# First attention: a head's maxima are turned into a row one step later, between that step's scores and values

## The chip, the cores and the metric

The kernel runs on one core of a Trainium2 chip. The metric is device time in microseconds (us) of one execution. Three executions of the kernel before took 3412.55, 3414.42 and 3423.49 us; their median, 3414.42 us, is the time before.

The core has five engines that run side by side and meet at semaphores: TensorE (PE, with its weight loads shown as PEld), VectorE (DVE), ScalarE (ACT), GpSimd (POOL) and SyncE (SP), which here only issues DMAs.

## The reference

The program is two transformer layers. Each layer is an attention and a feed-forward part, both with layer norms and residuals around them. Only the first attention is touched:

```python
B, S, H, NH = 2, 1024, 512, 16          # head width HD = 32
q, k, v = (proj(Wq), proj(Wk), proj(Wv))
q = q * cos + rotate_half(q) * sin      # k likewise
scores = jnp.einsum('bhqd,bhkd->bhqk', q, k) / math.sqrt(HD)
scores = jnp.where(causal, -jnp.inf, scores)
attn = jax.nn.softmax(scores, axis=-1)
out = jnp.einsum('bhqk,bhkd->bhqd', attn, v)
```

There are 32 heads (2 batches of 16) of 1024 queries by 1024 keys.

## The kernel before, in words

The first attention, `attention_layer0` (its tiles carry the prefix `l0a_`), treats one head after another. A head is worked on three times:

- **Maxima ("M").** The scores of a 128-query block are computed with the queries on the partitions, in parts of up to 512 keys: 12 parts in a head, widths 128, 256, 384, 512, 512+128, 512+256, 512+384, 512+512. PE writes a part into one of the two slots of `mbank` (L938, the causal mask by L941), and DVE reduces it to the negated maximum of each query (L1017). After the 12th part DVE joins the two halves of the blocks 4 to 7 into `negmax` (L1020, "the join").
- **The row ("N").** `negmax` is 128 x 8. PE transposes it (L948) into the next slot of `mbank`, DVE splits the 8 x 128 result into a rounded part and a rest (L1026, L1028), and SP copies both by DMA into two rows of `q_stack` (L894, L896). Against two rows of ones in `k_stack` they subtract each query's maximum inside the matmul.
- **Scores, exponentials, values ("Z", "L", "P", "O").** A head has six units. Z (L957, mask L960) computes a unit's scores with the keys on the partitions into one of two slots of `sbank`; ACT takes their exponential twice (L994 rounded, L995 in full); L on POOL subtracts one from the other for the rest (L1067, in four units of six); P (L981) multiplies with the values into `obank`; O on DVE copies and adds the finished half (L1036, L1039).

The order of the work is a list of steps, `steps_layer0`; each engine walks through the same list and does its own share. A head has six steps (k = 0 to 5). Step i does the scores of unit i + 2, the exponential rest of unit i, the values of unit i - 3, the copies that have become ready, and two maxima parts of the head after next. So during head h the row of head h + 1 is made (its maxima were finished in the last step of head h - 1), and the twelve maxima parts of head h + 2. The scores of head h + 1 start in step k = 4 of head h; they wait for the two DMAs of the row, which SP issues at its k = 2.

Two waits matter for what follows. The transpose waits for the join and for every reduction that stands before it in the list (`wait(pe, m_done, use["N", n])`). A maxima part waits until the part two places before it in the two slots of `mbank` has been reduced; the row takes one place in that sequence too.

Once in a group of four heads DVE inverts the group's sums (L1006), in the last step before its copies, and POOL then scales the group's output with them (L1058, twice), in step k = 1 of a head.

Of the kernel before, what the change touches and what calls it, by code (L numbers as in the profile page):

```python
# [734 lines left out]
HEADS = B * NH  # L735
# [31 lines left out]
def steps_layer0():  # L767

    for i in range(FIRST, LAST):
        h, k = divmod(i, U)  # L770
        if 0 <= i + 2 < HEADS * U:
            yield "Z", i, i + 2
        if k == 0 and 0 <= h + 1 < HEADS:
            yield "N", i, h + 1
        if 0 <= i < HEADS * U:
            yield "L", i, i
        p, o = i - LAG, i - LAG - 1
        if 0 <= p < HEADS * U:
            yield "P", i, p
        if 0 <= o < HEADS * U and o % U in (1, U - 1):  # L780
            yield "O", i, 2 * (o // U) + (o % U == U - 1)
        if h + 2 < HEADS:
            yield "M", i, 2 * (h * U + 2 * U + k)
            yield "M", i, 2 * (h * U + 2 * U + k) + 1


def uses_layer0():

    out, n = {}, 0
    for kind, _, e in steps_layer0():  # L790
        if kind in "MN":
            out[kind, e] = n
            n += 1
    return out


def attention_layer0(nc, m, ident, ident_bf, mask, qk_dram, v_dram, v32_dram, sums_dram, inverse_dram, out, next_load):
# [34 lines left out]
    with nc.Block() as block:  # L832
# [93 lines left out]
        def _(pe):  # L926
            pe.wait_ge(rows_set, 1)
            for kind, i, n in steps_layer0():
                if kind == "M":
                    h, part = divmod(n, len(MAX_PARTS))  # L930
# [54 lines left out]
        @block.scalar  # L985
        def _(act):
            for kind, i, n in steps_layer0():
                if kind == "Z":
                    _, _, wide = pieces(n % U)
                    r = n % RING0  # L990
                    act.wait_ge(scores_full, n + 1)
                    wait(act, values_done, n - RING0 + 1)
                    if n % U not in IN_FP32:
                        nc.scalar.activation(probs_hl[:, r, 0, 0:wide], sbank[:, n % 2, 0:wide], ACT.Exp)  # L994
                    nc.scalar.activation(probs[:, r, 0:wide], sbank[:, n % 2, 0:wide], ACT.Exp).then_inc(exp_done, 1)  # L995
# [1229 lines left out]
```

## Time and profile before

| | |
|---|---|
| median of three executions | 3414.42 us |
| profiled execution, its time | 3422.34 us |
| profiled execution, its span | 3420.6 us |
| PE busy over the span | 2878.7 us (84%) |
| DVE busy | 1944.4 us (57%) |
| ACT busy | 1184.9 us (35%) |
| POOL busy | 942.8 us (28%) |
| first attention | from 213 us to about 677 us of the span |
| mean granted TensorE clock | 0.927 |

Shares of the span are means over stages that are bound by different engines. The first attention fills slices 3 to 8 of the 40 of the page. A span that the trace calls busy on PE is modelled at its end; starts are what is measured, and intervals below are from start to start where that is possible.

### The profile page before, as it was taken

To read this page: it belongs to the slowest core of one execution; us is meant where nothing else is said; L and a number is where in the kernel's file an instruction comes from. 1 tells how busy PE (TensorE), PEld (TensorE's weight loads), DVE (VectorE), ACT (ScalarE), POOL (GpSimd) and SP (SyncE) were. 2 spreads that over 40 slices of the span, in tenths; PEclk is the share of its full clock that TensorE was granted. 3 is DMA by queue.
4 is the path that set the end of the run, shared out by engine and by line. 5 is a ranking of instruction groups with operands and counts; after the bars stand their busy time and mean duration, and the time that the engine had idled before them with its cause. 6 is when DMAs were issued, how large, how long until landed. Compare 5 with 4: busy or idle time off the path is not lost. (4 is left out here: it accounts for less than half of the span.)

```text
span 3420.6 us, 42283 instructions
## 1 busy us (share of the span) xinstructions
PE 2878.7 (84%) x14636; PEld 2300.5 (67%) x14636; DVE 1944.4 (57%) x3582; ACT 1184.9 (35%) x2287; POOL 942.8 (28%) x664
## 2 busy tenths in 40 slices
PE   7968888778999997358999999489999993588994
PEld 6846566556888885237888888468888882466773
DVE  5647777582223323345666666556666666766755
ACT  2226555532111111132444444224444442233331
POOL 1226666651111112104000000240000002277633
PEclk9979999988999998689999999799999996799997
DMA  4764333121100001760000000300000003111002
GB/s 171 238 190 123 112 106 110 48 99 56 37 19 19 18 1 64 245 270 27 22 21 32 21 32 17 151 27 22 21 32 21 32 17 135 37 37 37 0 1 98
DMA packets 123391, 236.96 MB, mean 69 GB/s; under 512 B 12832, under 2 KB 67104, under 8 KB 122496
## 3 DMA queue, kind: packets, MB, share of 16 engines
q1 hardware_dynamic: 123264, 235.32, 20.7%
q8 instruction: 73, 1.20, 0.2%
q14 instruction: 54, 0.44, 0.0%
HBM read 162.14 MB, written 72.88 MB: 69 GB/s over the span
## 5 line engine op out<-in xcount | busy, mean ns | idle before, releaser
L1067 POOL TENSOR_TENSOR l0a_probs_hl<-l0a_probs,l0a_probs_hl 128x896 fp32r<-128x896 f32 (+1 forms) x128 | 285.8, 2242 | 161.5 <-ACT l0a_probs L995 161.5
L1299 PE MATMUL l1a_obank<-l1a_pT_hl,l1k_v_hl 128*128 128x512 f32 (+3 forms) x1152 | 300.4, 370 | 7.2 <-DVE l1a_pT_hl L1372 7.1
L1372 DVE TENSOR_TENSOR l1a_pT_hl<-l1a_work,l1a_pT_hl 128x512 fp32r<-128x512 f32 (+3 forms) x384 | 213.1, 555 | 155.1 <-ACT l1a_pT_hl L1332 154.9
L1325 ACT ACTIVATE l1a_probs<-l1a_scores,l1a_row 128x128 f32<-128x128 f32 (+7 forms) x256 | 189.3, 741 | 318.0 <-DVE l1a_row L1362 318.0
L1279 PE MATMUL l1a_scores<-l1k_kT_hl,l1a_qa_hl 128*128 128x512 f32 (+3 forms) x1152 | 291.8, 362 | 1.5 <-ACT l1a_probs L1325 1.5
L1415 POOL TENSOR_TENSOR l1a_q_stage<-l1k_qpe,l1a_ones 128x512 fp32r<-128x512 f32 x32 | 33.3, 1040 | 875.9 <-PE l1a_work L1307 818.4
L1704 DVE TENSOR_TENSOR f0f_hid<-f0f_silu,f0f_ubank 128x512 f32<-128x512 f32 x64 | 44.1, 689 | 319.6 <-PE f0f_ubank L1639 319.6
L1332 ACT CAST l1a_pT_hl<-l1a_work 128x512 fp32r<-128x512 f32 (+3 forms) x384 | 183.5, 478 | 107.3 <-PE l1a_work L1290 106.1
L1307 PE MATMUL l1a_work<-l1a_wov,l1a_oT_hl 128*128 128x512 f32 x768 | 214.1, 401 | 5.0 <-DVE l1a_oT_hl L1391 3.0
L1362 DVE TENSOR_REDUCE l1a_row<-l1a_scores 128x1 f32<-128x128 f32 (+7 forms) x256 | 189.8, 751 | 44.7 <-PE l1a_scores L1282 44.6
L1759 POOL TENSOR_TENSOR f0f_h_hl<-f0f_hid,f0f_h_hl 128x512 fp32r<-128x512 f32 x64 | 82.7, 1292 | 475.6 <-ACT f0f_h_hl L1676 475.6
L1386 DVE SCALAR_TENSOR_TENSOR l_acc<-l1a_work,l1a_row,l_acc 128x512 f32<-128x512 f32 x256 | 189.4, 750 | 34.5 <-PE l1a_work L1307 25.3
L1279 PE MATMUL l1a_scores<-l1k_kpe,l1a_q_stack 128*128 128x512 f32 (+3 forms) x768 | 203.4, 346 | 0.0
L1279 PEld LDWEIGHTS l1a_scores<-l1k_kT_hl,l1a_qa_hl 128*128 128x128 f32 x1152 | 188.8, 191 | 21.7 <-ACT l1a_probs L1325 1.8
L1299 PEld LDWEIGHTS l1a_obank<-l1a_pT_hl,l1k_v_hl 128*128 128x128 f32 x1152 | 181.6, 191 | 28.8 <-DVE l1a_pT_hl L1372 14.9
L1290 PE MATMUL l1a_work<-all_ident,l1a_probs 128*128 128x128 f32 x1152 | 192.2, 276 | 9.5 <-DVE l1a_qa_hl L1377 6.2
L1639 PE MATMUL f0f_gbank<-x_xT,f0f_wT 128*128 128x512 f32 x768 | 190.6, 397 | 1.4 <-DVE f0f_wT L1698 1.4
L994 ACT ACTIVATE l0a_probs_hl<-l0a_sbank 128x896 fp32r<-128x896 f32 (+1 forms) x128 | 124.3, 971 | 190.1 <-PE l0a_sbank L957 115.9
L1649 PE MATMUL f0f_ybank<-f0f_wT,f0f_h_hl 128*128 128x512 f32 x768 | 189.8, 396 | 0.1
L1639 PE MATMUL f0f_ubank<-x_xT,f0f_wT 128*128 128x512 f32 x768 | 189.3, 395 | 0.0
L1649 PE MATMUL f1f_ybank<-f1f_wT,f1f_h_hl 128*128 128x512 f32 x512 | 139.6, 417 | 55.3 <-DVE f1f_h_hl L1708 36.4
L1290 PEld LDWEIGHTS l1a_work<-all_ident,l1a_probs 128*128 128x128 f32 x1152 | 140.6, 141 | 47.9 <-DVE l1a_qa_hl L1377 12.8
(258 smaller groups left out, 6255.3 us busy)
## 6 DMA issues: line engine op xcount, KB each, us to landing
v_dram<-l0f_v_rows SPq DMA_DIRECT2D x24, 768.0 KB, 4.3
qk_dram<-l0f_stage SPq DMA_DIRECT2D x128, 128.0 KB, 2.5
l1a_wov<-wov_dram SPq DMA_DIRECT2D x32, 512.0 KB, 3.4
l0a_v_stage<-v_dram SPq DMA_DIRECT2D x32, 384.0 KB, 4.3
l1a_wabs<-wabs_dram SPq DMA_DIRECT2D x32, 384.0 KB, 3.8
l0a_q_stack<-qk_dram SPq DMA_DIRECT2D x32, 256.0 KB, 3.5
l0a_k_stack<-qk_dram SPq DMA_DIRECT2D x32, 256.0 KB, 3.9
wov_dram<-w1a_wov SPq DMA_DIRECT2D x16, 512.0 KB, 3.3
```

The source lines that it names most:

```text
L1067: nc.gpsimd.tensor_tensor(probs_hl[:, r, 1, 0:wide], probs[:, r, 0:wide], f32(probs_hl[:, r, 0, 0:wide]), ALU.subtract).then_inc(low_done, 1)
L1279: last = pe.matmul(scores[:, buf, cols], lhs, rhs, start=(i == 0), stop=(not diagonal and i == len(steps) - 1))
L1290: last = pe.transpose(work[:, slot, i * P:(i + 1) * P], probs[s][:, first + n, :], ident[:, :])
L1299: last = pe.matmul(obank[:, c:SPAN], src["v_hl"][:, a, n, :], pT_hl[:, ring(n, s), b, c:SPAN], start=(n == 0 and i == 0), stop=(n == QT * ...
L1307: last = pe.matmul(work[:, slot, :], oT_hl[:, s, a, n * P:(n + 1) * P], wov[:, hp, b, :], start=(i == 0), stop=(i == 2))
L1325: nc.scalar.activation(probs[s][:, first:first + wide, :].rearrange("p k c -> p (k c)"), scores[:, n % S_AHEAD, 0:wide * P], ACT.Exp, bias ...
L1332: nc.scalar.copy(pT_hl[:, ring(n, s), 0, c:SPAN], work[:, slot, c:SPAN]).then_inc(turned_high, 1)
L1362: nc.vector.tensor_reduce(row[:, 0, row_slot:row_slot + 1], scores[:, n % S_AHEAD, 0:wide * P], AX.X, ALU.max, negate=True).then_inc(max_d ...
L1372: nc.vector.tensor_tensor(pT_hl[:, r, 1, c:SPAN], work[:, slot, c:SPAN], f32(pT_hl[:, r, 0, c:SPAN]), ALU.subtract).then_inc(work_free[slo ...
L1386: nc.vector.scalar_tensor_tensor(out=out[:, t, :], in0=work[:, slot, :], scalar=row[:, 2, row_slot:row_slot + 1], in1=out[:, t, :], op0=AL ...
L1639: last = pe.matmul(bank[:, b, :], wT[:, half, wa, w, c * HG + b * P:c * HG + (b + 1) * P], xT_hl[:, xa, c, a * SPAN:(a + 1) * SPAN], start ...
L1649: last = pe.matmul(ybank[:, b % 2, :], h_hl[:, a % 2, ht, ha, b * P:(b + 1) * P], wT[:, half, wa, 2, ht * D:(ht + 1) * D], start=(n == 0), ...
```

## The change

One line of the list of steps: the row of head h + 1 is yielded in step k = 1 of head h instead of step k = 0. Within a step it keeps its place, behind the scores and ahead of the values.

```diff
         if 0 <= i + 2 < HEADS * U:
             yield "Z", i, i + 2
-        if k == 0 and 0 <= h + 1 < HEADS:
+        if k == 1 and 0 <= h + 1 < HEADS:
             yield "N", i, h + 1
         if 0 <= i < HEADS * U:
             yield "L", i, i
```

PE, around the row, before. The first two rows are the last maxima parts of one head, then come the scores of step k = 0, the transpose (L948) and that step's values and maxima parts:

```order
L938 MATMUL l0a_mbank<-l0a_k_stack,l0a_q_stack 128x512 x2
L941 MATMUL l0a_mbank<-all_mask,all_ident_bf 128x128
L957 MATMUL l0a_sbank<-l0a_q_stack,l0a_k_stack 128x512 x2
L948 MATMUL l0a_mbank<-all_ident,l0a_negmax 8x128
L981 MATMUL l0a_obank<-l0a_probs_hl,l0a_v_stage 96x512 x4
L938 MATMUL l0a_mbank<-l0a_k_stack,l0a_q_stack 128x128
L941 MATMUL l0a_mbank<-all_mask,all_ident_bf 128x128
L938 MATMUL l0a_mbank<-l0a_k_stack,l0a_q_stack 128x256
L941 MATMUL l0a_mbank<-all_mask,all_ident_bf 128x128
L957 MATMUL l0a_sbank<-l0a_q_stack,l0a_k_stack 128x512 x2
```

PE at the same place, in the changed kernel:

```order
L938 MATMUL l0a_mbank<-l0a_k_stack,l0a_q_stack 128x512 x2
L941 MATMUL l0a_mbank<-all_mask,all_ident_bf 128x128
L957 MATMUL l0a_sbank<-l0a_q_stack,l0a_k_stack 128x512 x2
L981 MATMUL l0a_obank<-l0a_probs_hl,l0a_v_stage 96x512 x4
L938 MATMUL l0a_mbank<-l0a_k_stack,l0a_q_stack 128x128
L941 MATMUL l0a_mbank<-all_mask,all_ident_bf 128x128
L938 MATMUL l0a_mbank<-l0a_k_stack,l0a_q_stack 128x256
L941 MATMUL l0a_mbank<-all_mask,all_ident_bf 128x128
L957 MATMUL l0a_sbank<-l0a_q_stack,l0a_k_stack 128x512 x2
L948 MATMUL l0a_mbank<-all_ident,l0a_negmax 8x128
L981 MATMUL l0a_obank<-l0a_probs_hl,l0a_v_stage 96x512 x2
```

The transpose has moved behind one step's values, two maxima parts and the next step's scores.

DVE around the join, before (copies of O, the last two reductions, the join, the two splits of the row, the reductions of the next maxima parts):

```order
L1036 COPY l0a_o_rows<-l0a_obank 33x512
L1039 TENSOR_TENSOR l_oT<-l0a_obank,l0a_o_rows 32x512
L1017 TENSOR_REDUCE l0a_halves<-l0a_mbank 128x1 x2
L1020 TENSOR_TENSOR l0a_negmax<-l0a_halves 128x4
L1026 CAST l0a_negmax_hl<-l0a_mbank 8x128
L1028 TENSOR_TENSOR l0a_negmax_hl<-l0a_mbank,l0a_negmax_hl 8x128
L1017 TENSOR_REDUCE l0a_negmax<-l0a_mbank 128x1 x4
```

DVE at the same place, in the changed kernel:

```order
L1036 COPY l0a_o_rows<-l0a_obank 33x512
L1039 TENSOR_TENSOR l_oT<-l0a_obank,l0a_o_rows 32x512
L1017 TENSOR_REDUCE l0a_halves<-l0a_mbank 128x1 x2
L1020 TENSOR_TENSOR l0a_negmax<-l0a_halves 128x4
L1017 TENSOR_REDUCE l0a_negmax<-l0a_mbank 128x1 x2
L1026 CAST l0a_negmax_hl<-l0a_mbank 8x128
L1028 TENSOR_TENSOR l0a_negmax_hl<-l0a_mbank,l0a_negmax_hl 8x128
L1017 TENSOR_REDUCE l0a_negmax<-l0a_mbank 128x1 x2
```

The reductions of the maxima parts of step k = 0 (128 and 256 keys wide) now stand ahead of the two splits. The instructions of ACT, POOL and SP stand in the same order as before.

## Rows read from the trace of the kernel before

**Rows 1.** The page: granted TensorE clock in 40 slices.
```profile
PEclk9979999988999998689999999799999996799997
```
**Rows 2.** Busy time of each engine, 400 to 500 us; last columns clock, DMA share, GB/s.
```profile
400.00:500.00 100.00, 86.49 (x463) 60.08 (x464) 71.71 (x139) 58.50 (x72) 68.80 (x33) 0.95 0.38 111
```
**Rows 3.** Who waited for whom, 220 to 653 us: total, times, longest.
```profile
PE l0a_mbank L948 <- DVE l0a_negmax L1020: 53.3, 32, 2.6
```
**Rows 4.** Timeline of PE, the transpose alone: start, us, [idle before <-releaser].
```profile
233.48 0.37 PE L948 MATMUL l0a_mbank<-all_ident,l0a_negmax 128*8 128x128 f32 x1 [0.17 <-DVE l0a_negmax L1020]
...
400.53 0.27 PE L948 MATMUL l0a_mbank<-all_ident,l0a_negmax 128*8 128x128 f32 x1 [1.42 <-DVE l0a_negmax L1020]
413.46 0.28 PE L948 MATMUL l0a_mbank<-all_ident,l0a_negmax 128*8 128x128 f32 x1 [1.42 <-DVE l0a_negmax L1020]
426.78 0.27 PE L948 MATMUL l0a_mbank<-all_ident,l0a_negmax 128*8 128x128 f32 x1 [1.80 <-DVE l0a_negmax L1020]
442.44 0.38 PE L948 MATMUL l0a_mbank<-all_ident,l0a_negmax 128*8 128x128 f32 x1 [2.57 <-DVE l0a_negmax L1020]
456.76 0.27 PE L948 MATMUL l0a_mbank<-all_ident,l0a_negmax 128*8 128x128 f32 x1 [1.42 <-DVE l0a_negmax L1020]
...
652.07 0.27 PE L948 MATMUL l0a_mbank<-all_ident,l0a_negmax 128*8 128x128 f32 x1 [1.82 <-DVE l0a_negmax L1020]
```
**Rows 5.** Timeline, PE in the head from 400.53 us to 413.46 us.
```profile
401.67 0.36 PE L938 MATMUL l0a_mbank<-l0a_k_stack,l0a_q_stack 96*128 96x256 f32 x1
...
401.92 0.70 PE L957 MATMUL l0a_sbank<-l0a_q_stack,l0a_k_stack 98*128 98x512 f32 x2
...
402.46 0.97 PE L981 MATMUL l0a_obank<-l0a_probs_hl,l0a_v_stage 128*96 128x512 f32 x4
...
411.33 0.71 PE L957 MATMUL l0a_sbank<-l0a_q_stack,l0a_k_stack 98*128 98x512 f32 x2
```
**Rows 6.** Timeline, DVE in the same head and at its end.
```profile
401.90 0.67 DVE L1017 TENSOR_REDUCE l0a_negmax<-l0a_mbank 128x1 f32<-128x128 f32 x2 [0.47 <-PE l0a_mbank L941]
...
411.92 1.29 DVE L1017 TENSOR_REDUCE l0a_halves<-l0a_mbank 128x1 f32<-128x512 f32 x2
...
413.25 0.16 DVE L1020 TENSOR_TENSOR l0a_negmax<-l0a_halves 128x4 f32<-128x4 f32 x1
...
413.78 0.28 DVE L1026 CAST l0a_negmax_hl<-l0a_mbank 8x128 fp32r<-8x128 f32 x1 [0.37 <-PE l0a_mbank L948]
...
414.09 0.28 DVE L1028 TENSOR_TENSOR l0a_negmax_hl<-l0a_mbank,l0a_negmax_hl 8x128 fp32r<-8x128 f32 x1
```
**Rows 7.** Timeline, DVE and POOL, what comes once in four heads.
```profile
423.42 0.35 DVE L1006 RECIPROCAL l0a_sums<-l0a_sums 128x32 f32<-128x32 f32 x1
...
439.86 2.50 POOL L1058 TENSOR_TENSOR l_oT<-l_oT,l0a_inverse 128x512 f32<-128x512 f32 x2
...
441.07 1.32 DVE L1020 TENSOR_TENSOR l0a_negmax<-l0a_halves 128x4 f32<-128x4 f32 x1
```
**Rows 8.** Busy time in short stretches behind two long waits; columns as in rows 2.
```profile
424.90:428.30 3.40, 1.60 (x11) 1.17 (x11) 2.47 (x7) 1.94 (x2) 1.38 (x2) 1.00 0.01 1
428.30:431.70 3.40, 3.40 (x12) 2.20 (x11) 1.08 (x3) 1.94 (x2) 1.59 (x2) 0.52 0.29 82
```
**Rows 9.** The row's second DMA, its packets (DMA share by stretch), and the scores.
```profile
402.19 0.66 SPq L896 DMA_DIRECT2D l0a_q_stack<-l0a_negmax_hl  x1
...
403.35:403.75 0.40, 0.40 (x4) 0.21 (x2) 0.04 (x1) 0.40 (x2) 0.20 (x1) 1.00 0.04 10
403.75:404.20 0.45, 0.45 (x5) 0.25 (x4) 0.45 (x2) 0.45 (x1) 0.00 (x0) 1.00 0.00 0
...
407.24 0.48 PE L957 MATMUL l0a_sbank<-l0a_q_stack,l0a_k_stack 98*128 98x512 f32 x1
```
**Rows 10.** Timeline of POOL, one head and the last heads.
```profile
414.10 2.39 POOL L1067 TENSOR_TENSOR l0a_probs_hl<-l0a_probs,l0a_probs_hl 128x1024 fp32r<-128x1024 f32 x1 [2.03 <-ACT l0a_probs L995]
...
655.78 6.54 POOL L1067 TENSOR_TENSOR l0a_probs_hl<-l0a_probs,l0a_probs_hl 128x1024 fp32r<-128x1024 f32 x3 [1.07 <-ACT l0a_probs L995]
```

## The prediction

> **What bounds the kernel now.** I went from the page to the stage, then to its waits, then through one head instruction by instruction. The page gives PE the largest busy share, and the clock of slices 3 to 8, the first attention, is not at its full tenths [rows 1]. In that stage PE is busy 86.5% at a granted clock of 0.95, DVE 72%, POOL 69%, ACT 58% [rows 2]. So no engine but PE is near its limit, and PE loses 13.5 us in 100. The list of waits says where: the transpose of the maxima (L948) waits 32 times for the join (L1020), 53.3 us in all [rows 3]. No other wait of PE in the stage comes near that. Each head shows it once. A plain head lasts 12.93 us from transpose to transpose (400.53 to 413.46) and 1.42 us of it is this wait [rows 4]. The reason stands on DVE: it takes up the last two reductions at 411.92, ends them at 413.21 and joins until 413.41 [rows 6], while PE has issued the scores ahead of the transpose from 411.33 [rows 5].
>
> Two kinds of head are worse. Once in four heads DVE inverts the group's sums (0.35 us) on the way to the join [rows 7], and the wait is 1.80 us (seven such heads, the last at 652.07) [rows 4]. In the next head POOL scales (439.86 to 442.36), and the join, 0.16 us elsewhere, takes 1.32 us and ends with it [rows 6, 7]; the wait is 2.57 us (six such heads, 2.54 to 2.57) [rows 4].
>
> The clock belongs to the same wait. Behind the stall of 1.80 us the granted clock goes from 1.00 to 0.52, which is the lower level, 1.2 GHz, with some of the edge in it [rows 8]; behind the 2.57 us stall it does so again, and behind the 1.42 us ones it stays at 2.4 GHz. In time: the head after the 1.80 us stall lasts 15.66 us (426.78 to 442.44). A plain head with the stretched join would last 12.93 + (1.32 - 0.16) = 14.09, so the drop costs 1.57. The next one lasts 14.32 against 12.93, so that drop costs 1.39 [rows 4].
>
> **What the change removes.** The transpose no longer stands between the scores of k = 0 and that step's values. PE goes straight on. In the plain head: scores of k = 0 start at 411.33 and take 0.54 (from 401.92 to the next instruction at 402.46), so the values start at 411.87 instead of 413.50 [rows 5].
>
> **What takes its place.** From the transpose to the second maxima part is 401.67 - 400.53 = 1.14 us [rows 4, 5], of which the transpose itself holds PE some 0.03. PE therefore reaches the second part at 411.87 + 1.11 = 412.98. That part now needs the slot of the last part of the head before, whose reduction ends at 413.21 [rows 6]; with the 0.06 that the transpose now needs behind the join (413.41 to 413.46) it starts at 413.27: a new wait of 0.3 us. The scores of k = 1 start 0.25 later (401.67 to 401.92), at 413.52, and end at 414.06. Then comes the transpose. It waits for all reductions ahead of it in the list, and these now include the two parts just issued. DVE: join until 413.41, then both reductions back to back, 0.67 us and a gap of 0.04 on each side [rows 6], so until 414.15. The transpose starts at 414.21, a second new wait of 0.15, and the values of k = 1 at 414.25. Before, they started at 402.46 + 12.93 = 415.39. **The gain is 1.14 us a head, and a plain head lasts 11.79 us.** 0.28 us of the 1.42 us are waited elsewhere.
>
> From the values of k = 1 on nothing else in the head changes its place, and every duration to the next join is as now. DVE has the splits still to do at that point: they start 0.32 and 0.63 behind the transpose [rows 4, 6], so they end at 415.12, and the next reduction cannot start before about 415.5. Nobody waits for them but the fourth maxima part, which PE reaches at about 415.3, and the row's DMAs.
>
> The two special heads keep their extras, since these sit on DVE ahead of the join or in it: 0.38 for the inversion, 1.16 for the join behind POOL's scaling. With the latter the transpose waits 0.15 + 1.16 = 1.3 us. The step's gain of 1.14 is the same there. So the stall part is 29 heads by 1.14 = 33 us; I leave out the heads of the two ends, where the wait at 233.48 is only 0.17 [rows 4].
>
> The Trainium skill (SBUF — State Buffer, "Who interferes with whom") says that a DVE instruction with two SBUF inputs is blocked for the whole of a GpSimd instruction that reads SBUF. The join is one, the reductions out of PSUM are not; by that rule the 1.16 us stays where it is, and the danger is a join that slips under the next GpSimd instruction (a rival below).
>
> **The clock.** The longest wait of a plain head is then 0.3 and of an inverting head 0.3 + 0.38 = 0.7; neither is near 1.42, which does not bring the clock down. The scaling head has 1.3 us behind 0.3 us, 0.8 apart. One by one they are under 1.42; together, 1.6 lies between what leaves the clock alone and what does not. I take the value that the single wait is nearest to, no drop. Before there are twelve drops, six of 1.57 and six of 1.39 (two in each of six groups of four heads): 17.8 us. The bounds are 0 and 17.8.
>
> The Trainium skill (TensorE: Matmul & The Clock Gate, "Why this matters for your kernels") asks only that there be no idle gaps over some 3 us. By that rule a 1.80 us wait would not cost the clock, the drops would have another cause and would stay; the sum would be 34 and not 52 us. The trace speaks against it, with a drop behind each stall of 1.80 us within the stage, though none behind the last, at 652.07.
>
> **The end of the stage.** Behind the last transpose there are no maxima parts. POOL idles 1.07 us at 655.78 for the exponential of the scores that now come before the transpose, and then runs 6.54 us without a gap [rows 10]. That 1.07 goes: 1 us.
>
> **The row's DMAs.** They lose the most slack. Now the second is issued at 402.19 and the scores that need it start at 407.24; its last packets fall in 403.35 to 403.75, none after [rows 9]. In the changed kernel the last split starts 414.84, the first DMA is issued 0.31 later, the second at 415.9. Its packets end by 417.5. The scores need it at 407.24 - 402.46 + 414.25 = 419.03. 1.5 us are left. Price between 0 and, if the landing needed all of today's 5.05 us, 5.05 - 3.13 = 1.9 us a head; the packets say 0.
>
> **Sum.** 33 + 17.8 + 1 = 52 us of the profiled 3422.34, so 3370. The median of the runs is 7.9 us under the profiled execution; from it, 3414.4 - 52 = 3362.
>
> **The rivals.**
> 1. *Part of the clock stays* (the scaling head's 0.3 and 1.3 us count together, or one of the two drops in a group stays). Six to seven drops at 1.4 are 9 us: 3371. For: PE was busy 1.60 of the 3.40 us before the drop at 428.30 [rows 8], and the scaling head would come close to that. Against: 1.42 us alone never sufficed.
> 2. *None of the clock comes back*: the drops have another cause. Stall and end only, 34 us: 3380. Against: where they stand.
> 3. *The wait only moves.* PE then waits elsewhere for DVE or POOL, and the head stays at 12.9 us. For: DVE would be busy about 9.3 of 11.79 us (72% of 12.93), the highest share but PE's. Against: the gaps on DVE left in a head, over 1 us ahead of the third part. No change, 3414.
> 4. *More than counted*: the low clock at the stage's start ends sooner, or the inversion finds a gap: some 10 us more, 3352.
> 5. *Slower: the join slips under POOL.* It ends at 413.41, and POOL starts its 2.39 us subtraction at 414.10 [rows 6, 10]; the join of an inverting head ends 0.3 us before. If the shorter head brought the join past that start, it would be held to 416.49, both reductions to 417.2, and the values of k = 1 to 417.3 against 415.39: 1.9 us more a head, 29 heads, +56 us, 3470. It decides once the join moves 0.85 us relative to POOL. Against: both hang on the same PE instructions (scores of k = 0), which keep their distance. In the inverting heads alone it would cost 7 x 2.3 = 16 us of the gain.
>
> **How the numbers follow.** Forecast 3362: 0.49. Rival 1: 0.19, rival 2: 0.13, rival 3: 0.07, rival 4: 0.08, rival 5: 0.04. The forecast's own uncertainty is 5 us for the runs' spread. 3350 to 3384 takes in rivals 1, 2 and most of 4, and leaves some 0.17 out. Telling a change from none needs about 0.3%, 10 us here: faster 0.89, same 0.07, slower 0.04.
>
> **What would show it.** In the trace after: transposes 11.8 us apart in a plain head; the wait of the transpose for a reduction (L1017) near 0.15 us and not for the join, except about 1.3 us in one head of four; a new wait near 0.3 us at the second maxima part, and 0.7 in the inverting head; the clock at 1.00 throughout 250 to 600 us; no wait of L957 for the DMA of L896. Wrong would be: plain heads over 12.3 us, a join of over 1 us in more than one head of four, or clock drops in heads without a long wait.

## The result, and the profile after

The changed kernel took 3367.76 us (median of four runs, 3365.83 to 3370.76) beside 3417.88 us for the kernel before: a ratio of 0.9854, 95% interval 0.9834 to 0.9874. That is 50 us less; 3362 with a range of 3350 to 3384 was forecast. Of the 5.8 us between 3362 and 3367.8, 3.5 are that the kernel before took 3417.88 us here and not 3414.42, and 2 that 50 us came off and not 52. Measured again beside other runs of before, it was 3370.57 against 3413.64, a ratio of 0.9865 (0.9847 to 0.9882). The profiled execution took 3367.46 us, its span is 3365.7 us against 3420.6.

The page's granted clock, against [rows 1]. Slices 4 to 7, which lie in the first attention, are 9 before and after: a 9 stands for 90% or more, so the page can't show the drops in this stage. The next view can.

```profile
PEclk9969999879999997789999999799999995799997
```

The stage's busy time, against [rows 2] (same columns), shows all engines denser in the same 100 us, PE at 97.9% and the clock at 1.00:

```profile
400.00:500.00 100.00, 97.91 (x541) 67.18 (x540) 80.53 (x160) 67.86 (x83) 78.63 (x38) 1.00 0.45 133
```

Who PE waited for in the first attention, 240 to 595 us (total us, times, longest), is the answer to [rows 3]. The wait for the join is gone from the list, and what is left in PE's own rows is 1 us. The new waits stand in the rows of the weight loads (PEld), 29 and 58 times in these heads:

```profile
PE l0a_mbank L938 <- DVE l0a_halves L1017: 1.0, 6, 0.2
PEld l0a_mbank L948 <- issue: 14.3, 29, 0.5
PEld l0a_mbank L938 <- DVE l0a_halves L1017: 13.0, 58, 0.3
```

The transposes, against [rows 4] (timeline of PE; start, us). The idle time before them is no longer attributed to a releaser, except before the last one:

```profile
406.69 0.27 PE L948 MATMUL l0a_mbank<-all_ident,l0a_negmax 128*8 128x128 f32 x1
...
418.68 0.27 PE L948 MATMUL l0a_mbank<-all_ident,l0a_negmax 128*8 128x128 f32 x1
430.66 0.27 PE L948 MATMUL l0a_mbank<-all_ident,l0a_negmax 128*8 128x128 f32 x1
442.64 0.27 PE L948 MATMUL l0a_mbank<-all_ident,l0a_negmax 128*8 128x128 f32 x1
455.01 0.27 PE L948 MATMUL l0a_mbank<-all_ident,l0a_negmax 128*8 128x128 f32 x1
...
599.05 0.27 PE L948 MATMUL l0a_mbank<-all_ident,l0a_negmax 128*8 128x128 f32 x1 [0.41 <-DVE l0a_negmax L1020]
```

A plain head lasts 11.98 us (430.66 to 442.64) and not 12.93; an inverting head 12.37 (442.64 to 455.01); the head that ends at 418.68, in which POOL scales, 11.99 and not 15.66 (the 15.66 held a clock drop too). There is no head over 12.4 us behind the start of the stage, and the clock record has no drop between 250 and 622 us.

PE, DVE and POOL around one transpose (one timeline, against [rows 5, 6]; this head is a scaling one):

```profile
415.68 0.71 PE L957 MATMUL l0a_sbank<-l0a_q_stack,l0a_k_stack 98*128 98x512 f32 x2
416.22 1.10 PE L981 MATMUL l0a_obank<-l0a_probs_hl,l0a_v_stage 128*96 128x512 f32 x4
416.27 1.29 DVE L1017 TENSOR_REDUCE l0a_halves<-l0a_mbank 128x1 f32<-128x512 f32 x2
416.39 2.53 POOL L1058 TENSOR_TENSOR l_oT<-l_oT,l0a_inverse 128x512 f32<-128x512 f32 x2
...
417.59 0.16 DVE L1020 TENSOR_TENSOR l0a_negmax<-l0a_halves 128x4 f32<-128x4 f32 x1
417.61 0.19 PEld L938 LDWEIGHTS l0a_mbank<-l0a_k_stack,l0a_q_stack 96*128 96x128 f32 x1 [0.27 <-DVE l0a_halves L1017]
417.61 0.39 PE L938 MATMUL l0a_mbank<-l0a_k_stack,l0a_q_stack 96*128 96x256 f32 x1
...
417.88 0.71 PE L957 MATMUL l0a_sbank<-l0a_q_stack,l0a_k_stack 98*128 98x512 f32 x2
418.11 0.42 DVE L1017 TENSOR_REDUCE l0a_negmax<-l0a_mbank 128x1 f32<-128x256 f32 x1 [0.16 <-PE l0a_mbank L941]
...
418.65 0.08 PEld L948 LDWEIGHTS l0a_mbank<-all_ident,l0a_negmax 128*8 128x8 f32 x1 [0.49 <-issue]
...
420.34 0.66 SPq L896 DMA_DIRECT2D l0a_q_stack<-l0a_negmax_hl  x1
```

The values of k = 0 follow the scores at once. The second maxima part starts 0.05 us behind the end of the last long reduction (416.27 + 1.29 = 417.56), with 0.27 us of waiting in front: the first of the two new waits. The scores of k = 1 take 0.54, to 418.42, the reduction of the part just issued ends at 418.53, and the transpose's weights load at 418.65: the second new wait, about 0.25 us. The trace calls it "issue", though it is a wait for DVE, as an experiment below shows. The surprise stands in the scaling row: the join starts in the middle of POOL's scaling and takes 0.16 us, where it took 1.32 us before [rows 7].

### The profile page after: what moved, and what is told of

Its sections match the earlier page's. It is cut to its first block and busy times, and to the rows that moved or that the text cites. A ratio compares the mean times of both kernels' runs of the same rounds, so it can differ in the third digit from the quotient of the medians.

```text
span 3365.7 us, 42283 instructions
## 1 busy us (share of the span) xinstructions
PE 2872.0 (85%) x14636; PEld 2292.9 (68%) x14636; DVE 1936.0 (58%) x3582; ACT 1185.6 (35%) x2287; POOL 943.1 (28%) x664
## 5 line engine op out<-in xcount | busy, mean ns | idle before, releaser
L1067 POOL TENSOR_TENSOR l0a_probs_hl<-l0a_probs,l0a_probs_hl 128x896 fp32r<-128x896 f32 (+1 forms) x128 | 285.2, 2249 | 107.1 <-ACT l0a_probs L995 107.1
```

The lines of the kernel that those rows point to most:

```text
L1067: nc.gpsimd.tensor_tensor(probs_hl[:, r, 1, 0:wide], probs[:, r, 0:wide], f32(probs_hl[:, r, 0, 0:wide]), ALU.subtract).then_inc(low_done, 1)
```

## The experiments

Each was compared with the kernel before in the same session; the sessions' medians of before were 3414.1, 3420.3 and 3413.6 us. "In the trace" means between the first and the last transpose: 429.6 us before, 375.2 us after.

### Is the clock the stall's doing?

The first three leave the row at k = 0. b_both takes both extras off the way to the join, b_scale and b_invert one each.

```diff
@@ DVE, before.py        (b_invert, b_both)
-                if kind == "P" and late == 6 and 0 <= group < GROUPS - 1:
+                if kind == "P" and late == 7 and 0 <= group < GROUPS - 1:
                     invert(group)
@@ POOL, before.py       (b_scale, b_both)
-                if kind == "P" and late == 14 and 0 <= group < GROUPS - 1:
+                if kind == "P" and late == 15 and 0 <= group < GROUPS - 1:
                     scale(group)
```

**b_both.** 

> The kernel before, with the row where it was (k = 0), but the two extras taken off the way to the join: POOL scales one step later (k = 2), DVE inverts the sums in the gap behind the splits of the row (k = 0 of the next head). Theory (the clock falls behind stalls of 1.80 us and more): every stall is 1.42 us, every head 12.93 us, the clock stays at 1.00 from 250 us to 650 us, no join over 0.2 us. That takes off 17.8 us of clock, 6 x 1.16 us of join and 7 x 0.38 us of inversion: 27 us. Rival (the drops have another cause): the drops stay, 9.6 us are gained.

Measured: 3398.03 us, ratio 0.9948 (0.9932 to 0.9964). In the trace the theory holds. PE timeline and the busy time of the stage (columns as in rows 2):

```profile
404.26 0.27 PE L948 MATMUL l0a_mbank<-all_ident,l0a_negmax 128*8 128x128 f32 x1 [1.42 <-DVE l0a_negmax L1020]
417.20 0.27 PE L948 MATMUL l0a_mbank<-all_ident,l0a_negmax 128*8 128x128 f32 x1 [1.41 <-DVE l0a_negmax L1020]
```
```profile
250.00:625.00 375.00, 334.06 (x1887) 232.74 (x1886) 281.08 (x559) 238.04 (x290) 273.68 (x129) 1.00 0.38 111
```

All 29 heads behind the start last 12.91 to 12.95 us, each with a stall of 1.40 to 1.50 us ahead of it, and the clock does not fall once from 244 us to the end of these heads. First to last transpose is 400.9 us, 28.6 less than before (27 expected). So the twelve drops hang on the stalls of 1.80 us and more, and they are worth 28.6 - 7.0 (join) - 2.7 (inversion) = 18.9 us with the start of the stage, of which its first two heads are 0.6. The rival is refuted. But the time fell by 16 us only, where 27 were expected; the part on the rest of the program takes that up.

**b_scale.** 

> The kernel before with POOL's scaling one step later alone. Theory: the join is 0.16 us in every head, the 2.57 us stall becomes 1.42 us and the drop behind it goes; the 1.80 us stall and its drop stay. 6 x 1.16 + 6 x 1.39 = 15 us less. Rival (the second drop follows from the first and not from the join): 7 us less, twelve drops.

Measured: 3404.91 us, ratio 0.9971 (0.9958 to 0.9984), 9 us less where 15 were expected. No join over 0.27 us, no stall over 1.80 us, no drop at a scaling head: theory, and the rival falls. In the trace it is 21.0 us less and not 15, mostly because only four of the seven stalls of 1.79 to 1.80 us have a drop behind them. Two of the seven, and what follows each (timeline of PE; busy time, columns as in rows 2):

```profile
313.26 0.27 PE L948 MATMUL l0a_mbank<-all_ident,l0a_negmax 128*8 128x128 f32 x1 [1.79 <-DVE l0a_negmax L1020]
...
366.96 0.27 PE L948 MATMUL l0a_mbank<-all_ident,l0a_negmax 128*8 128x128 f32 x1 [1.79 <-DVE l0a_negmax L1020]
```
```profile
314.00:317.00 3.00, 3.00 (x12) 2.15 (x11) 0.88 (x3) 0.94 (x2) 1.89 (x1) 0.57 0.04 12
...
368.00:371.00 3.00, 3.00 (x20) 2.08 (x18) 1.52 (x4) 1.90 (x2) 1.62 (x1) 1.00 0.13 46
```

The same stall in the same instructions, once with the clock at the lower level behind it and once not. The length alone does not decide at 1.8 us.

**b_invert.** 

> The kernel before with the inversion in the gap behind the splits of the row alone. Theory: no stall of 1.80 us, six drops behind the 2.57 us ones stay (the join still meets the scaling): 7 x 0.38 + 6 x 1.57 = 12 us less. Rival (the clock counts something longer than one head): more or fewer drops than six.

Measured: 3409.75 us, ratio 0.9989 (0.9979 to 0.9999), 4 us less where 12 were expected. Its profiled execution was the fastest of its ten (3403.95), with a span 18 us under that of before; first to last transpose is 15.1 us shorter. In the trace five joins are held for 1.30 us and one is not; behind the five stalls of 2.54 to 2.55 us the clock falls five times, behind the sixth head's 1.42 us it does not. So there are five drops and not six, and the sixth is missing because its stall is. One of the five and the sixth (timeline of PE):

```profile
490.49 0.27 PE L948 MATMUL l0a_mbank<-all_ident,l0a_negmax 128*8 128x128 f32 x1 [2.55 <-DVE l0a_negmax L1020]
...
543.78 0.27 PE L948 MATMUL l0a_mbank<-all_ident,l0a_negmax 128*8 128x128 f32 x1 [1.42 <-DVE l0a_negmax L1020]
```

Stalls and drops over the traces of before and these three, from 244 us on: 1.40 to 1.51 us, never a drop (95 stalls); 1.79 to 1.82 us, ten of fourteen; 2.54 us and more, eleven of eleven.

### The join and POOL's scaling

**a_one_scale**: the changed kernel, and POOL scales in one instruction.

```diff
-                for s in range(2):
-                    rows = out[:, group, s * SPAN:(s + 1) * SPAN]
-                    nc.gpsimd.tensor_tensor(rows, rows, inverse[:, group % 2, s * SPAN:(s + 1) * SPAN], ALU.mult
-                                            ).then_inc(scaled, 1)
+                rows = out[:, group, 0:2 * SPAN]
+                nc.gpsimd.tensor_tensor(rows, rows, inverse[:, group % 2, 0:2 * SPAN], ALU.mult
+                                        ).then_inc(scaled, 2)
```

> The changed kernel with POOL's scaling as one instruction over 1024 columns (2.5 us) instead of two over 512. Theory (in the changed kernel the join slips in between the two scalings, by some 30 ns): the join starts about 1.2 us into the one instruction and is held until its end, 1.3 us, in six heads; the transpose there waits about 1.4 us; 7 us slower than the changed kernel, clock unchanged. Rival A (the scaling no longer touches the join in the changed kernel for another reason): the same time as the changed kernel. Rival B (the 0.27 us wait ahead counts with it): six clock drops more, 15 us slower.

Measured: 3374.05 us, ratio to before 0.9879 (0.9858 to 0.9901); 6.3 us over the changed kernel's first median (another session; the first-to-last stretch of the trace is 3.1 us longer, with 1.5 us less at the start of the stage). DVE, POOL and PE of one scaling head:

```profile
417.33 1.20 DVE L1020 TENSOR_TENSOR l0a_negmax<-l0a_halves 128x4 f32<-128x4 f32 x1
```
```profile
416.12 2.38 POOL L1057 TENSOR_TENSOR l_oT<-l_oT,l0a_inverse 128x1024 f32<-128x1024 f32 x1
```
```profile
419.21 0.27 PE L948 MATMUL l0a_mbank<-all_ident,l0a_negmax 128*8 128x128 f32 x1 [0.88 <-DVE l0a_negmax L1017]
```

The join starts at 417.33 and ends with the scaling, 416.12 + 2.38 = 418.50: held to its end, six times of six. The transpose's idle time is then 0.88 us in the list where it was 0.09, the head lasts 12.78 and not 11.98, and there is no clock drop. Theory, with 6 x 0.8 = 4.8 us where 7 was said; both rivals fall, and with B the worry of the prediction that the scaling head's wait would cost the clock.

**after_again**: the changed kernel once more. 

> The changed kernel once more, beside the runs of the same chip: the time of its first runs (3368) within 3 us. Theory (a join that meets the boundary between the two scalings falls either way): its six joins need not be the 0.16 us of the first trace; each may be 0.16 or 1.3. Rival (the boundary always falls one way in this kernel): six times 0.16 us.

Measured: 3370.57 us, 2.8 over the first runs, and so within the 3. Five joins are as in the first trace; one is not (timeline of POOL and DVE):

```profile
512.99 2.53 POOL L1058 TENSOR_TENSOR l_oT<-l_oT,l0a_inverse 128x512 f32<-128x512 f32 x2
...
514.20 1.34 DVE L1020 TENSOR_TENSOR l0a_negmax<-l0a_halves 128x4 f32<-128x4 f32 x1
```

The join asks at the boundary between the two scalings. In the changed kernel, before, b_invert and two kernels below it starts 0.00 to 0.05 us ahead of the second one; it gets in between, or it waits for the second too. Before it lost six times of six, in the changed kernel it won six of six and five of six, in b_invert it won one of six, in a_relax and a_invert (below) three of six each. At 0.02 us ahead or less it lost eleven of eleven, at 0.03 to 0.05 it won 18 of 25; the seven that it lost there all have 0.04, and so have several that it won. So what decides is not seen in the starts. Where a join asked 0.26 us ahead (a_k2, below), it took 0.32 us and got in six times of six. That the join mostly goes through in the changed kernel was not designed, and a lost one costs 0.85 to 1.16 us: 7 us between before and after.

**a_scale**: the changed kernel with the scaling at k = 2 (the edit of b_scale). 

> The changed kernel with POOL's scaling one step later (k = 2). Theory: the join is free of it already, so the time is that of the changed kernel within 2 us. Rival (the scaling costs something else there, POOL's backlog at the next exponential rests): 3 to 7 us faster.

Measured: 3369.05 us, ratio 0.9849 (0.983 to 0.9868); its joins take 0.16 to 0.27 us. The same as the changed kernel within the noise, as the theory has it: its first-to-last stretch, 373.9 us, is 1.2 us shorter, and the first two heads account for that.

### What the new waits are

**a_relax**:

```diff
-                    wait(pe, m_done, use["N", n])
+                    wait(pe, m_done, use["N", n] - 1)
```

> The changed kernel with the transpose waiting only for the reduction two places back in the slots of mbank (and for the join, as now), not for the one just ahead of it. Theory (the transpose's wait in the changed kernel is for the second of the two parts of k = 0): the 0.26 us wait goes, a plain head lasts 11.7 us, 29 x 0.26 = 7.5 us less than the changed kernel, 3360. Rival (DVE sets the pace of the head, and what PE saves here it waits at the next parts): the same time as the changed kernel, PE waiting longer for L1017 elsewhere.

Measured: 3364.83 us, ratio 0.983 (0.9811 to 0.985), 3 us under the changed kernel's first median; no run of the changed kernel was taken beside it, and by the ratios it is 8 us, so the time alone decides little. The trace does: first to last transpose is 370.9 us and not 375.2. PE in a head whose join went through:

```profile
415.66 0.71 PE L957 MATMUL l0a_sbank<-l0a_q_stack,l0a_k_stack 98*128 98x512 f32 x2
416.21 0.27 PE L948 MATMUL l0a_mbank<-all_ident,l0a_negmax 128*8 128x128 f32 x1
```

The transpose follows the scores after 0.55 us, where it was 0.80 in the changed kernel, and a plain head lasts 11.74 and not 11.98. So the 0.25 us called "issue" was the wait for the reduction, and DVE does not take it back. That is 7 us over the stage; three joins that lost (0.85 us a head) give back 2.6 of them.

**a_invert**: the inversion at k = 1 (`late == 8`), its store at SP's k = 2 (`late == 9`). 

> The changed kernel with the inversion of the sums in DVE's gap behind the splits of the row (k = 1) and its store behind the row's DMAs on SP. Theory: the 0.38 us that seven heads last longer go, 2.7 us less. Rival: nothing, because the inversion now delays the reductions behind it by as much.

Measured: 3370.33 us, ratio 0.9845 (0.9825 to 0.9865): nothing gained that the noise would show. Not by the rival: the inverting heads do last 11.98 us like the others. Three joins lost against the scaling and cost 0.93 us each (12.91), 2.8 us, what the inversion brought.

### How far the row can move

**a_k2**: `k == 2` in place of `k == 1`. 

> The row yet another step later (k = 2). Theory (the row's DMAs still have 1.5 us in hand at k = 1): a step later they have not. The splits end some 1.0 us behind a transpose at about 2.4 us past the values of k = 1, the second DMA is issued at 4.0 us, its packets end at 5.5 us, the scores that need it stand at 4.8 us: PE waits for the DMA in every head, 1 to 1.5 us, so 30 to 45 us slower than the changed kernel, 3400 to 3415. Rival (the landing is faster than the packets' end suggests, or the scores slip anyway): within 5 us of the changed kernel.

Measured: 3386.21 us, ratio 0.9894 (0.9875 to 0.9913): 18 us slower than the changed kernel by the medians (14 by the ratios, 18.7 between the first and the last transpose), less than forecast. Its waits of PE, 240 to 595 us, then one head:

```profile
PE l0a_sbank L957 <- DMA l0a_q_stack<-l0a_negmax_hl: 11.5, 27, 0.4
PE l0a_mbank L948 <- DVE l0a_negmax L1017: 8.6, 27, 0.3
```
```profile
407.77 0.66 SPq L896 DMA_DIRECT2D l0a_q_stack<-l0a_negmax_hl  x1
```
```profile
409.59 0.50 PE L957 MATMUL l0a_sbank<-l0a_q_stack,l0a_k_stack 98*128 98x512 f32 x1 [0.42 <-DMA l0a_q_stack<-l0a_negmax_hl]
```

A head lasts 12.65 us, 0.67 more; both waits together are 0.74. The scores start 1.82 us behind the issue of the second DMA (407.77 to 409.59): that is the row's landing. The mechanism is the one named; the size was off because the scores get to their place late by themselves: the DMA was issued 4.2 us behind the values of k = 1 (403.55), close to the 4.0 expected, but the scores, without their wait, would have started 5.6 us behind them and not 4.8.

### A version that beats both

**a_best**: a_relax, a_scale and a_invert together. 

> The changed kernel with three of the edits together: the transpose waits two places back only, POOL scales at k = 2, DVE inverts behind the splits (its store behind the row's DMAs). Theory (the three are independent): every head lasts 11.74 us, the inverting ones too, and no join is over 0.3 us, since the scaling is not near it any more; 29 x 0.24 + 7 x 0.38 = 9.6 us less in the first attention than the changed kernel, about 3358. Rival (what is gained in the stage is spent by later stages, or the inversion delays a reduction now that the head is shorter): the attention is 9.6 us shorter in the trace, but the time is within 5 us of the changed kernel.

Measured: 3359.16 us (five runs, 3357.57 to 3364.1), ratio 0.9836 (0.982 to 0.9852), 11 us under the changed kernel of the same session (3370.57) and the best measured. Behind the start, all heads but the last last 11.72 to 11.75 us. One point of the theory was wrong: six joins take 0.47 to 0.48 us (by the tail of POOL's backlog, L1067, which ends 0.3 us later in those heads), and no head is longer for it, since PE's second part does not wait for the join. Stretch of the stage, columns as in rows 2:

```profile
250.00:595.00 345.00, 340.94 (x1910) 239.46 (x1910) 282.73 (x559) 241.86 (x296) 277.51 (x132) 1.00 0.41 122
```

PE is busy 98.8% of it. What could still be saved in this stretch between PE's instructions is 4 us. In the trace the first-to-last stretch is 10.0 us shorter than in the changed kernel's first trace, where 9.6 were expected.

## Why the prediction was right, point by point

From the first to the last transpose the trace lost 54.4 us, 429.6 to 375.2. But the transpose itself has moved against the work around it, so the terms are better counted between the scores of k = 0 and the last values of the stage, which are the same instructions in both. The last values end at 673.3 us before and at 619.1 in the changed kernel, 54.2 earlier: 52.9 of it in the 29 heads (the 27.6, 7.0 and 18.3 of the table), 1.15 behind the last of those scores and 0.1 at the start. The span fell by 54.9, with 0.7 behind the stage.

| term | predicted | measured |
|---|---|---|
| the stall, 29 heads | 29 x 1.14 = 33 | 29 x 0.95 = 27.6 |
| the join behind the scaling | 0 | 6 x 1.16 = 7.0 |
| the clock | 17.8 | 18.3, by b_both |
| end of the stage | 1 | 1.15 (23.74 to 22.59 us) |
| in the time | 52 | 50 (43 beside the second set) |

- **What bounds the kernel** was read rightly: PE, and the join ahead of the transpose. Only the first sentence on the clock reads more out of [rows 1] than they hold: their 9s in the stage may be full; the 0.95 of [rows 2] is what shows the loss. With the wait gone PE is at 97.9%, and DVE, POOL and ACT rise to 68 to 81% without setting the pace.
- **The second maxima part's wait** was right to 0.03 us: 0.27 where 0.3 was said. The part starts 1.93 us behind the scores of k = 0 (415.68 to 417.61); 1.94 was worked out.
- **The transpose's second wait** was mis-sized. From the part to the transpose it takes 1.07 us and not 0.94. The reductions were not back to back: the 256-wide one waits 0.16 us for its part, starts 0.50 behind it (417.61 to 418.11) and ends at 418.53, 0.92 behind it where 0.88 was worked out. And the transpose starts 0.15 behind that end, where the 0.06 between the join and the transpose had been used. a_relax shows that it is this wait.
- **"Every duration to the next join is as now"** was not quite so: the values of k = 1, now directly behind the transpose, take 0.89 us to the next part (418.71 to 419.60) and took 0.80 (402.46 to 403.26). The values of k = 0, which stood behind the transpose before, took 1.00 us to the next part then (400.56 to 401.57) and take 0.93 now: the surcharge has moved, and the prediction left it where it was. These two misses, 0.13 and 0.09, are why a plain head lasts 11.98 us and not 11.79.
- **The special heads.** The inversion kept its 0.38. That the join would go on being held by POOL's scaling was wrong: the step that failed is "the two special heads keep their extras". The rule of the Trainium skill (SBUF — State Buffer, "Who interferes with whom") was applied as if the join met one instruction of 2.5 us; it meets two of 1.26 to 1.29 at their boundary. a_one_scale shows the rule itself at work: a two-input DVE instruction held to the end of the GpSimd instruction that reads SBUF, here 1.20 us. In the sum that step left out 7.0 us that went. It also meant that the wait of 1.3 us in the scaling head, on which rival 1 rests, did not occur in the changed kernel; a_one_scale has a wait of 0.88 us there and no drop. That this failure and the two above nearly cancel (7.0 against 5.4 us) is luck.
- **The clock** came back whole, and b_both shows that the stall was the cause and not the row's place. It was worth 18.3 and not 17.8, since the trace of before has three of its six second drops at 1.6 us (heads of 14.51 to 14.53) and not at 1.39. The rule of the Trainium skill (TensorE: Matmul & The Clock Gate, "Why this matters for your kernels"), no gaps over some 3 us, does not hold here as a sufficient one: stalls of 2.54 us cost the clock eleven times of eleven, 1.80 us often. Rivals 1 and 2 fall, and rival 3 too: the head is 0.95 us shorter. Of rival 4 there is next to nothing: 0.1 us at the start of the stage, none from the inversion.
- **The row's DMAs**: 1.5 us of slack were left by the prediction. In the trace the second is issued at 420.34 and the scores that need it come 11.98 us behind those at 411.60, at 423.58; with a landing of 1.82 us (a_k2), 1.4 us were left.
- **The slower rival** never came near: the join kept its distance to POOL's subtraction in plain heads, and no join there is over 0.3 us.

**The rest of the program.** The experiments' times do not follow their traces' stages to better than 10 us. Behind the last values of the first attention the same instructions follow in all of these kernels (but for POOL's last scaling in a_one_scale), and they lasted from 2744.0 us (b_invert) to 2755.3 us (b_scale): 2747.3 before, 2746.6 after, 2749.9 in b_both; after_again and a_best, of one session, have 2750.1 and 2749.3. Here are before and b_scale, from about 2 us behind their last transposes to the end:

```profile
654.00:3420.60 2766.60, 2324.26 (x11823) 1896.13 (x11821) 1514.18 (x2729) 880.76 (x1880) 613.52 (x488) 0.93 0.15 52
```
```profile
632.60:3409.70 2777.10, 2335.10 (x11824) 1904.40 (x11823) 1514.82 (x2729) 882.25 (x1880) 614.16 (x488) 0.92 0.15 52
```

As many instructions to within two, 10.5 us more, PE 11 us busier at a slightly lower mean clock, DVE, ACT and POOL as busy as before to 1.5 us. Of the 10.5 us, 2.5 lie still in the end of the attention, where b_scale has a drop behind its last stall, and 8.0 behind it. By the clock records the stretch behind the attention has 405 us at the lower level in before and 431 us in b_scale; over the twelve traces the shortest of these stretches (2744.0) has the least, 401 us, and the longest the most. So the difference goes with the clock. What makes those drops come or go is not shown. It may be that the waits of the later stages fall at other moments when a stage ends earlier, or that it differs from execution to execution: the eight executions of b_scale spread over 13 us (3398 to 3411), and the profiled one was the longest. b_scale's first-to-last stretch is 21.0 us shorter than before's and its span 10.9: these 10.5 us. b_both's is 28.6 shorter and its span 23.4: of the 5.2 us between the two, 4.6 lie behind the last transpose. What the medians differ beyond that lies within the spread of the runs of before, 3408 to 3429 us. No run tried the moment by itself (a delay put ahead of the later stages would).

## What to carry to other kernels

When two engines hand work back and forth, look where the waiting engine could already do the next item of its own list, and put the hand-over behind it: here one step of distance took 1.4 us out of every head and only 0.5 came back as new waits. Move it no further than the next consumer allows (k = 2 cost 18 us), and check that the wait asks for no more than it needs (0.25 us a head). Value a stall of PE with the clock that goes with it: of 54 us saved in the stage a third was the clock, and taking only the extras off the path (b_both) won that third in the stage without touching the other stalls, though only 16 of its 28.6 us showed in the median.

## What the runs showed of the hardware that was not expected

- A DVE instruction of 0.16 us with two SBUF inputs was held until the end of a GpSimd instruction that had started before (1.20 us by one of 2.38 us). When it asked within 0.05 us ahead of the boundary between two GpSimd instructions, it got in or had to wait for the second one too (1.29 to 1.34 us), differently in two executions of the same kernel.
- The granted clock fell behind ten of fourteen stalls of 1.79 to 1.82 us and eleven of eleven of 2.54 us or more, never behind the 95 of 1.40 to 1.51 us, in a stage that otherwise kept PE busy. What distinguishes the ten from the four is open.
- A wait of PE whose releaser had ended 0.1 us before was listed as "issue" (0.25 us, a wait for DVE as a_relax shows).
- Values right behind a transpose of 128 x 8 took 0.07 to 0.09 us longer than the same values elsewhere (0.89 against 0.80 us, 1.00 against 0.93).
